# Two-layer block with attention and experts: the rotation of the last two groups moved from VectorE to GpSimd, and their value projections put ahead of their query projections

## What is computed

```
xn = layernorm(x)
x  = x + attention0(xn) + experts(xn)
xn = layernorm(x)
x  = x + attention1(xn) + channel_mix(xn)
```

## Time and profile before

| | |
|---|---|
| median of 3 runs | 362.1 us (361.76 to 363.16) |
| profiled execution, its time | 362.24 us |
| profiled execution, its span | 360.4 us |
| PE busy | 344.5 us, 96% |
| DVE busy | 322.7 us, 90% |
| ACT busy | 273.5 us, 76% |
| POOL busy | 210.1 us, 58% |

### The profile page before, as it was taken

The page is one execution under the profiler, slowest core; times in us unless marked ns, Lnnn a source line. Parts: engine busy times, 40 slices in busy tenths (PEclk is TensorE's granted clock), DMA queues, the critical chain, the costliest instruction groups (busy, mean ns, idle before and its releaser), DMA issues.

```text
span 360.4 us, 9159 instructions
## 1 busy us (share of the span) xinstructions
PE 344.5 (96%) x2496; PEld 299.6 (83%) x2496; DVE 322.7 (90%) x635; ACT 273.5 (76%) x759; POOL 210.1 (58%) x231
## 2 busy tenths in 40 slices
PE   8899769999999999999999999999999899999996
PEld 3788325499999999999999999999999688788885
DVE  3997889969999999999799989998996799998665
ACT  3888846687787878787878777887995987777851
POOL 3899100682334466866776768877877458883110
PEclk9999979999999999999999999999999999999999
DMA  6932846564445455556545554565552102220011
GB/s 186 231 107 79 320 196 193 181 157 128 128 133 151 122 160 147 156 143 171 167 148 147 162 156 140 156 170 153 151 137 75 31 0 60 59 61 29 29 31 58
DMA packets 45520, 46.96 MB, mean 130 GB/s; under 512 B 6928, under 2 KB 33712, under 8 KB 45216
## 3 DMA queue, kind: packets, MB, share of 16 engines
q1 hardware_dynamic: 40288, 36.88, 34.4%
q0 software_dynamic: 4320, 8.86, 10.1%
q10 hardware_dynamic: 864, 0.66, 0.7%
HBM read 32.86 MB, written 13.50 MB: 129 GB/s over the span
## 4 chain that ended last, share of the span: by engine, by line
PE 81%; issue 9%; DVE 4%; ACT 2%; DMA 2%; POOL 0%; DVEq 0%; POOLq 0%
PE banks L530 18%; PE banks L517 17%; PE banks L656 7%; PE banks L657 7%; PE banks L968 3%; PE banks L501 2%; PE banks L332 2%; PE banks L997 2%; PE banks L1044 2%; PE banks L1026 2%; PE banks L1006 2%; PE banks L732 2%; PE banks L978 2%; PE banks L1014 2%; PE banks L323 2%
## 5 line engine op out<-in xcount | busy, mean ns | idle before, releaser
L445 POOL DMA_INDIRECT xg<-xn_rows,slot_tok x71 | 78.6, 1106 | 82.9 <-PE banks L501 42.0
L547 ACT ACTIVATE xT<-banks,b1T 128x128 f32<-128x128 f32 x284 | 81.3, 374 | 18.1 <-PE banks L517 17.0
L462 POOL DMA_INDIRECT qk_exp<-expert_rows,ranki x64 | 74.5, 1165 | 19.1 <-issue 18.5
L530 PE MATMUL banks<-w_sb,xT 128*128 x568 | 79.0, 282 | 0.0
L517 PE MATMUL banks<-xgT,w 128*128 128x128 f32 x568 | 75.4, 276 | 0.0
L530 PEld LDWEIGHTS banks<-w_sb,xT 128*128 128x128 f32 x568 | 69.4, 192 | 0.6
L517 PEld LDWEIGHTS banks<-xgT,w 128*128 128x128 f32 x568 | 69.0, 192 | 0.5 <-issue 0.5
L668 DVE TENSOR_TENSOR cq<-banks,phi 128x360 f32<-128x360 f32 (+1 forms) x96 | 47.4, 549 | 7.0 <-PE banks L657 6.4
L640 DVE TENSOR_TENSOR low<-outer,high 128x1152 fp32r<-128x1152 f32 x32 | 43.5, 1358 | 5.3 <-ACT high L634 5.1
L634 ACT CAST high<-outer 128x1152 fp32r<-128x1152 f32 x32 | 37.0, 1156 | 10.8 <-DVE outer L623 9.2
L677 DVE TENSOR_REDUCE sums<-cq 128x144 f32<-128x1152 f32 x32 | 43.1, 1347 | 0.1
(11 more groups left out here) (206 smaller groups left out, 696.8 us busy)
## 6 DMA issues: line engine op xcount, KB each, us to landing
w<-in_L_ffn_W SPq DMA_DIRECT2D x71, 256.0 KB
expert_rows<-ye SPq DMA_DIRECT2D x71, 64.0 KB
expert_rows<-x_sb SPq DMA_DIRECT2D x2, 2048.0 KB, 9.6
x_sb<-in_L_attn_x SPq DMA_DIRECT2D x8, 256.0 KB, 3.9
xn_rows<-xn SPq DMA_DIRECT2D x8, 256.0 KB, 2.4
w_sb<-in_L_ffn_W SPq DMA_DIRECT2D x8, 256.0 KB, 3.8
out<-outer SPq DMA_DIRECT2D x7, 256.0 KB, 2.3
xg<-xn_rows,slot_tok POOLq DMA_INDIRECT x71
```

The source lines that it names most:

```text
L445: pool.indirect_dma_start(out=xg[n][:, :], out_offset=None, in_=xn_dram, in_offset=bass.IndirectOffsetOnAxis(ap=slot_tok[:, j:j + 1], axis ...
L462: pool.indirect_dma_start(out=y_moe[:, i, k, :], out_offset=None, in_=y_dram, in_offset=bass.IndirectOffsetOnAxis(ap=ranki[:, 0, k, i:i + ...
L530: last = nc.tensor.matmul(y, hidT[p][:, c, :], w2_sb[:, ds(e * NC + c, 1), :], start=False, stop=(c == NC - 1))
L547: last = nc.scalar.activation(hidT[p][:, c, :], slot_bank(j)[:, c * P:(c + 1) * P], ACT.Gelu_apprx_tanh, bias=b1T[:, ds(e * NC + c, 1)])
```

## The change

- Groups 6 and 7 are now `BY_POOL`. VectorE has nothing of their rotation any more: two halves of products and two sums of each group leave it. ScalarE copies each half of raw queries and keys from its PSUM bank to SBUF (`raw_queries`, semaphore `qk_raw`), in all four copies of 128x512. GpSimd makes the products from the copies (`rope_products_pool`, two instructions of 128x512 for each half, in all eight) and then the sums with its `rope_sum` (four instructions).
- TensorE projects the values of groups 6 and 7 first, and the queries of both behind them. The second half-pair waits for ScalarE's copies, since the banks are the same.
- ScalarE has no exponential ahead of the last values any more. After them it makes the four copies, then the late weights, then groups 0 to 5 (six in place of five), then waits for the slot numbers. Groups 6 and 7 stay behind the one-hot rounds and now wait for GpSimd.
- The semaphores of `deviation` are merged to one that counts in threes.

```diff
+    BY_POOL = (NG - 2, NG - 1)
     def queries1_tensor(pe, g, h, p):
-        if g:
+        if g > BY_POOL[0]:
+            pe.wait_ge(qk_raw, (g - BY_POOL[0] - 1) * 2 + h + 1)
+        elif g:
             pe.wait_ge(rope_ready, g * 2 + h - 1)
...
     def rope_sum(pool, g):
-        pool.wait_ge(rope_ready, g * 2 + 2)
+        if g in BY_POOL:
+            pool.wait_ge(rope_pool, 4 * (BY_POOL.index(g) + 1))
+        else:
+            pool.wait_ge(rope_ready, g * 2 + 2)
...
-    BY_VECTOR = (NG - 2, NG - 1)
-
-    def rope_sum_vector(v, g, f):
-        v.wait_ge(rope_ready, g * 2 + 2)
-        a, b = rope_terms(g, f)
-        nc.vector.tensor_tensor(a, a, b, ALU.add).then_inc(rot_last, 1)
+    def raw_queries(act, g, h):
+        n = BY_POOL.index(g) * 2 + h
+        act.wait_ge(qk_ps, g * 2 + h + 1)
+        nc.scalar.copy(qkv3[:, ds(g * GT + 2 * h, 2), 0:2 * D], ps[4 + h].rearrange("p (t c) -> p t c", t=2)
+                       ).then_inc(qk_raw, 1)
+
+    def rope_products_pool(pool, g, h):
+
+        n = BY_POOL.index(g) * 2 + h
+        pool.wait_ge(qk_raw, n + 1)
+        raw, sines = (a[:, ds(g * GT + 2 * h, 2), 0:2 * D].rearrange("p t (h d) -> p t h d", d=DH)
+                      for a in (qkv3, qk_exp))
+        nc.gpsimd.tensor_tensor(sines, raw, by_position("sin"), ALU.mult).then_inc(rope_pool, 1)
+        pool.wait_ge(rope_pool, 2 * n + 1)
+        nc.gpsimd.tensor_tensor(raw, raw, by_position("cos"), ALU.mult).then_inc(rope_pool, 1)
...
@@ scalar
-                if g == NG - 2:
-                    exp_relu(act, 0)
+            for g in BY_POOL:
+                for h in range(2):
+                    raw_queries(act, g, h)
...
-            for g in range(1, NG - 2):
+            for g in range(BY_POOL[0]):
                 exp_relu(act, g)
@@ gpsimd
             for g in range(NG):
-                if g not in BY_VECTOR:
-                    rope_sum(pool, g)
+                if g in BY_POOL:
+                    for h in range(2):
+                        rope_products_pool(pool, g, h)
+                rope_sum(pool, g)
@@ tensor
             for g in range(NG):
                 values1_tensor(pe, g, g % 2)
-                queries1_tensor(pe, g, 0, g % 2)
+                if g < BY_POOL[0]:
+                    queries1_tensor(pe, g, 0, g % 2)
                 if g + 1 < NG:
                     xT_tensor(pe, g + 1, 1 - g % 2)
-                queries1_tensor(pe, g, 1, g % 2)
+                if g < BY_POOL[0]:
+                    queries1_tensor(pe, g, 1, g % 2)
+            for g in BY_POOL:
+                for h in range(2):
+                    queries1_tensor(pe, g, h, g % 2)
...
-            pe.wait_ge(rope_ready, NG * 2)
+            pe.wait_ge(qk_raw, 4)
             attn_tokens_bank(pe)
@@ vector
-            for g in range(NG - 1):
+            for g in range(BY_POOL[0]):
                 for h in range(2):
                     rope_products(v, g, h)
...
             choose()
             TS(one_mu[:, :], mu[:, :], -1.0, 1.0, ALU.mult, ALU.add)
-            rope_sum_vector(v, NG - 2, 0)
...
-            rope_products(v, NG - 1, 0)
             v.wait_ge(tab_ps, NG)
...
-            rope_sum_vector(v, NG - 2, 1)
-            rope_products(v, NG - 1, 1)
-            for f in range(2):
-                rope_sum_vector(v, NG - 1, f)
             v.wait_ge(gate_exp, 1)
```

More of the change, by code:

```diff
@@ L223, in build @@
     zeros_ready = sem("zeros_ready")
-    ln_stats, ln_mv, ve_ready, rstd_part, shift_part, rstd_ready, xn_ready = (
+    ln_stats, ln_mv, deviation_step, rstd_ready, xn_ready = (
         [sem(f"{name}{layer}") for layer in range(2)]
-        for name in ("ln_stats", "ln_mv", "ve_ready", "rstd_part", "shift_part", "rstd_ready", "xn_ready"))
+        for name in ("ln_stats", "ln_mv", "deviation_step", "rstd_ready", "xn_ready"))
     xT_ps, xT_ready = sem("xT_ps"), sem("xT_ready")
@@ L236, in build @@
         sem("hot_ready"), sem("hot_by_tile"), sem("hot_by_row"), sem("tab_ps"), sem("exp_ps"), sem("exp_ready"), sem("idx_ready"))
-    rope_ready, rot_ready, rot_last, exp_part, phi_parts, phi_ready = (
-        sem("rope_ready"), sem("rot_ready"), sem("rot_last"), sem("exp_part"), sem("phi_parts"), sem("phi_ready"))
+    rope_ready, rope_pool, rot_ready, exp_part, phi_parts, phi_ready = (
+        sem("rope_ready"), sem("rope_pool"), sem("rot_ready"), sem("exp_part"), sem("phi_parts"), sem("phi_ready"))
+    qk_raw = sem("qk_raw")
     xg_in = [sem(f"xg_in{n}") for n in range(NX)]
@@ L274, in deviation @@
         pool.wait_ge(ln_mv[layer], g + 1)
[L275 to L280, removed]
+        nc.gpsimd.tensor_tensor(ve[n][:, :], mv[n][:, :, 1], eps4[:, :], ALU.add).then_inc(deviation_step[layer], 1)
+        pool.wait_ge(deviation_step[layer], 3 * g + 1)
+        nc.gpsimd.tensor_tensor(rstd[n][:, :], ve[n][:, :], mhalf[:, :], ALU.pow).then_inc(deviation_step[layer], 1)
+        pool.wait_ge(deviation_step[layer], 3 * g + 2)
+        nc.gpsimd.tensor_tensor(minus[n][:, :], mv[n][:, :, 0], rstd[n][:, :], ALU.mult).then_inc(deviation_step[layer], 1)
+        pool.wait_ge(deviation_step[layer], 3 * g + 3)
         nc.gpsimd.tensor_tensor(shift[n][:, :], zero4[:, :], minus[n][:, :], ALU.subtract).then_inc(rstd_ready[layer], 1)
@@ L385, in rope_sum @@
         last.then_inc(rot_ready, 1)
-    BY_VECTOR = (NG - 2, NG - 1)
-    def rope_sum_vector(v, g, f):
-        v.wait_ge(rope_ready, g * 2 + 2)
-        a, b = rope_terms(g, f)
-        nc.vector.tensor_tensor(a, a, b, ALU.add).then_inc(rot_last, 1)
+    def raw_queries(act, g, h):
[11 more added lines that the diff above has]
+        nc.gpsimd.tensor_tensor(raw, raw, by_position("cos"), ALU.mult).then_inc(rope_pool, 1)
     def exp_relu(act, g):
[L396 to L399, removed]
+        act.wait_ge(rot_ready, g + 1)
         nc.scalar.activation(qk_exp[:, ds(g * GT, GT), :], qkv3[:, ds(g * GT, GT), 0:2 * D], ACT.Exp).then_inc(exp_part, 1)
@@ L1346, in _ @@
             nc.scalar.activation(row(6), row(1), ACT.Exp).then_inc(gate_exp, 1)
-            for g in BY_VECTOR:
+            for g in BY_POOL:
                 exp_relu(act, g)
```

## The result

| | median | range | ratio to before |
|---|---|---|---|
| before, 4 runs | 362.09 us | 361.76 to 363.16 | |
| changed, 4 runs | 370.56 us | 370.23 to 371.04 | 1.0235 (1.0214 to 1.0255) |

The account below looks back on a forecast made before the run. VectorE's chain up to `slot_tok` was taken as the bound; 4.6 us late at `choose`, less 0.1, plus 1.85 behind it gave 6.3 us on 362.24: 368.5, as median 368.4 us, range 364.5 to 373.5.

Parts of the forecast that it names:

- likeliest case: Whole kernel: 366.6 to 370 us, from GpSimd holds of 1.05 to 1.20 us and up to 0.7 us from the clock.
- The bound: VectorE's chain from 36.5 to 64.6 us sets when `slot_tok` is ready; the kernel's end moves one for one with it.
- The start of the choice: VectorE's `choose` starts at 35.2 us for 36.46, 1.3 us earlier, which buys nothing because GpSimd sets the pace.
- The collision in the choice: In `choose`, eight two-input VectorE instructions alternate with GpSimd's in rounds of 1.41 us; it ends at 47.4 us, 4.6 late.
- Behind the choice the sum: After `choose`: 0.1 us given back, three blocked VectorE instructions cost 1.85 us; first one-hot at 56.0 us, 6.3 late in all.
- GpSimd's instructions: GpSimd's products and sums of 128x512 were taken at 1.25 us each.
- rival b: GpSimd's products are dearer, or GpSimd wins twice in a row now and then: 371.5 to 374 us, chance 0.12.
- TensorE's clock: A recovered clock at the turn gives up to 0.7 us, a slower count costs 0.1 us; nothing was taken.
- ScalarE: Four copies and six groups end at 51.8 us, before the delayed slot numbers, so ScalarE is not late.
- rival (a): Mild collision: GpSimd lets VectorE in, VectorE starts 1.3 us early, ScalarE is last at the slot numbers; 361.0 us, chance 0.13.
- the 1.1 us that I gave it: Gain without the collision: VectorE comes 1.4 us earlier, less 0.2 to 0.3 us for a late ScalarE.
- The rule of the Trainium skill: Two-SBUF-input VectorE instructions and GpSimd's SBUF reads exclude each other for a whole instruction; without it, a gain of 1.1 us.

Follow-up runs that it names:

- a_again: Changed kernel without GpSimd's twelve new instructions (groups 6 and 7 unrotated), run a second time: 361.89 us, 1.0006 times the kernel before.
- h_again: Kernel before with group 0's exponential behind the late weights and two products of zeros for six, run a second time: 361.14 us, ratio 0.9970.
- b_writes_only: Changed kernel with GpSimd's twelve new instructions turned into memsets of the same size: 385.99 us, 1.0002 times the kernel before.
- e: Changed kernel with each of GpSimd's twelve new instructions cut into two of 128x256: 394.53 us, 1.0186 times the kernel before.
- f_one_mu: Changed kernel with the two-element tensor_scalar behind the choice moved behind the slot list: 399.24 us, 1.0303 times the kernel before.
- a_pool_idle: Changed kernel without GpSimd's twelve new instructions (groups 6 and 7 unrotated), first run: 386.70 us, 1.0034 times the kernel before.
- g_pool_later: Changed kernel with GpSimd's twelve new instructions held back until the choice is over: 398.53 us, 1.0311 times the kernel before.

## Why the prediction was right, and where it was off

- **The result as a whole.** The time lies in the forecast band (366.5 to 371.5 us), by the mechanism that was forecast. It lies 0.6 us above the likeliest case (366.6 to 370), since the loss was 8.5 us for 6.3.
- **The bound.** Right. The end followed the list of slots: 8.23 us at `slot_tok`, 8.65 at the first transposes, 8.8 in the span. For small changes it follows less closely: a_again has its list 0.7 us earlier and gains nothing, h_again 1.5 us earlier and gains 0.7.
- **The start of the choice.** 35.2 us was forecast, 35.42 measured. That it buys nothing was right: GpSimd sets the pace.
- **The collision in the choice.** Right in kind and size: behind the first instruction, eight rounds of 1.41 us. It ended at 47.77 us for 47.4. The first instruction ended 0.35 us later than reckoned (36.45 for 36.1), and so did all.
- **Behind the choice the sum was too low.** It had 0.1 us given back between the choice and the scan, and 1.85 us for three blocked instructions. Measured against before: the gap from the choice's end to the scan went from 0.60 to 1.07 us (+0.47), L1586 cost +0.42, the scan L1589 +0.94 for 0.45, L1591 +0.94, L1597 +0.50. Together 3.27 us where the sum had 1.75; with the 4.96 us of the choice that is 8.23 us, and the forecast was 6.3. Two readings were wrong here. The sum counts ten of fourteen GpSimd instructions done when the choice ends, but one for the first instruction and one for each of the eight rounds are nine; five were left. And it let only instructions with two SBUF inputs be blocked, three of them. Five were, as many as GpSimd had instructions left. Two of the five have one input: the tensor_scalar L1580 (1.23 us for 0.16) and L1586 (0.59 for 0.17); b, e and f show instructions of this kind blocked too (0.48, 0.69 and 0.94 us), b by writes. L1580 by itself cost little, as f_one_mu shows: without it the list came 0.2 us earlier at most.
- **GpSimd's instructions.** 1.25 us was taken; undisturbed they took 1.27 and 1.28 (L409 at 50.21 us, above), in turns 1.33 to 1.47. Dear products (rival b) are ruled out: they cost what the sums cost.
- **TensorE's clock.** I took nothing and said up to 0.7 us. The counting matmul ran at the low clock (granted 0.50, behind 5.86 us of idle; before 1.00, behind 2.61) and took 0.62 us for 0.40. In f_one_mu, without L1580, the gap to the scan is 0.71 us for 0.60 before: 0.1 us for the clock, as was said, and the rest of the 0.47 us is L1580. At the turn the clock was low again, with VectorE waiting 0.72 us, as before.
- **ScalarE.** Ready at 52.05 us, 51.8 forecast. In a_pool_idle, the case of rival (a), VectorE waited for it by 0.30 us, as that rival had it; in a_again it did not, and there, where the end can be read, no gain reached it (list 0.7 us earlier, ratio 1.0006). So even without the collision the change was worth less than the 1.1 us that I gave it.
- **The rule of the Trainium skill** ("SBUF — State Buffer", "Who interferes with whom"), by which GpSimd's reads exclude VectorE instructions with two SBUF inputs and its writes don't: by it the kernel was to become slower, as it did, and b_writes_only agrees: the same instruction takes 0.42 us beside a memset (L1565 at 37.68 us) and 1.40 us beside a product in the changed kernel (L1560 at 37.90 us).
  The same section also counts copy, cast and tensor_scalar among what can block, when their operands meet the conditions of the modes that use both ports, and that is a part that I left out of the sum. The trace agrees: 1.23 us for 0.16 at L1580, 1.19 us for 0.20 at the cast of g_pool_later.

## What to carry to other kernels

Where VectorE is the bound, look at what stands there on VectorE before elementwise work goes to an idle GpSimd: what counts is how many of VectorE's instructions fall into GpSimd's busy time and are of a kind that waits. In this kernel each of them waited for up to one whole GpSimd instruction, be it of 8 elements or 512. Before moving work there, look in the trace for one place where the two already overlap, and compare that VectorE instruction with its like. VectorE's work from PSUM (the products of the projection, 0.69 us beside GpSimd's sums) and its reductions kept their times beside GpSimd. A chain of tiny dependent instructions was no better place than the choice: the list came 8.3 us late in g_pool_later, 8.2 in the changed kernel. Cutting GpSimd's instructions in half brought the first one-hot instruction 1.9 us forward (56.01 for 57.92) and no more, since the shorter waits fell on more of VectorE's instructions.

## What the runs showed of the hardware

- The same program found TensorE at either clock behind the same idle time. In a_pool_idle the turns followed 3.32 us of idle at a granted clock of 1.00 (2.4 GHz), in a_again, on another chip, also behind 3.32 us, at 0.50 (1.2 GHz); one trace of each doesn't tell whether the chip has to do with it. The windows of 49 to 51 us, a_pool_idle first, then a_again (the columns are those of rows 9):

```profile
49.00:51.00 2.00, 2.00 (x12) 0.94 (x12) 1.93 (x6) 1.97 (x3) 0.00 (x0) 1.00 0.25 100
```

```profile
49.00:51.00 2.00, 2.00 (x6) 0.97 (x7) 1.93 (x6) 1.97 (x3) 0.00 (x0) 0.50 0.25 102
```

  Six products of zeros take 1.46 us in the one and 2.77 in the other, and the list starts at 63.02 and 63.60 us. So half a microsecond at such a place can't be put down to an edit from one trace.
- A reduction and an instruction with one input in PSUM kept their times beside GpSimd in every run (0.42 us, and 0.69 to 0.70 us for the scan over the counts).
